# Where cross-attention's residual is added: on VectorE from the bank, or by TensorE in the bank as a product with the unit matrix

## The reference

```python
corr = irfft(rfft(q) * conj(rfft(k))).mean(-1)        # per head, over the 512 tokens
weights, delays = top_k(corr, 6)
w = softmax(weights)
out = sum over the 6 delays of w * v rolled by the delay
...
return out @ Wo.T + bo
...
x = _layernorm(x + _L0_xattn_ref(x, ctx_1024, ctx_1024, ...), axis=-1)
```

## Time and profile before

| | us |
|---|---|
| median of 3 runs | 681.18 |
| lowest, highest | 680.11, 685.95 |
| the profiled execution | 685.06 |
| its span (first to last instruction) | 683.3 |
| TensorE busy in it | 581.0 |
| VectorE busy | 464.7 |
| ScalarE busy | 281.6 |
| last row of stage 4 written by ScalarE, from the span's start | 560.59 |
| first instruction of stage 5 | 560.89 |

### The profile page before, as it was taken

One profiled execution on the slowest core, in us unless ns is written; L12 is line 12 of the kernel. 1 busy time (PEld: TensorE's weight loads), 2 busy tenths in 40 slices (PEclk: granted clock), 3 DMA queues, 4 the chain that ended last, 5 costly groups with the idle time before them and its releaser, 6 DMA issues. The chain is left out here.

```text
span 683.3 us, 16712 instructions
## 1 busy us (share of the span) xinstructions
PE 581.0 (85%) x7318; PEld 418.9 (61%) x7318; DVE 464.7 (68%) x898; ACT 281.6 (41%) x510; POOL 117.6 (17%) x102
## 2 busy tenths in 40 slices
PE   5886889899998989988878767799999758998984
PEld 2454567677767668766434445688787644655642
DVE  2885857857776786865688799354566854676674
ACT  1756544433442443423443532343324054544531
POOL 1001520340061034000201225272000010000000
PEclk9998989999999999999999898899999878999998
DMA  6600710320151022214310007000000000000001
GB/s 178 214 3 0 228 53 4 126 95 4 34 156 35 4 74 85 65 64 155 125 31 0 32 32 236 31 1 1 0 1 1 0 0 1 1 29 3 32 14 48
DMA packets 26535, 37.48 MB, mean 55 GB/s; under 512 B 4641, under 2 KB 13602, under 8 KB 26463
## 3 DMA queue, kind: packets, MB, share of 16 engines
q1 hardware_dynamic: 26463, 36.42, 16.5%
HBM read 34.31 MB, written 2.10 MB: 53 GB/s over the span
## 5 line engine op out<-in xcount | busy, mean ns | idle before, releaser
L298 DVE SCALAR_TENSOR_TENSOR arena<-bank,conv_w,arena 128x511 f32<-128x511 f32 (+2 forms) x72 | 53.2, 746 | 18.5 <-ACT arena L457 13.9
L1522 POOL COPY arena<-v_win 128x256 f32<-128x256 f32 x32 | 20.4, 664 | 170.6 <-PE bank L775 170.5
L1974 ACT COPY arena<-bank 128x512 f32<-128x512 f32 x40 | 23.3, 584 | 55.6 <-PE bank L1777 36.9
L1777 PE MATMUL bank<-v_win,arena 128*128 128x256 f32 x192 | 45.7, 387 | 0.0
L2549 PE MATMUL bank<-v_win,arena 128*128 128x256 bf16 x288 | 36.5, 279 | 7.9 <-DVE arena L2636 6.9
L775 PE MATMUL bank<-arena 128*32 128x128 f32 x512 | 35.7, 409 | 6.4 <-ACT arena L1139 4.5
L1777 PEld LDWEIGHTS bank<-v_win,arena 128*128 128x128 f32 x192 | 37.1, 195 | 5.6 <-issue 0.4
L1189 ACT COPY arena<-bank 128x512 f32<-128x512 f32 x40 | 21.6, 589 | 45.3 <-PE bank L901 45.3
L1759 PE MATMUL bank<-v_win,arena 128*128 128x256 f32 x128 | 33.1, 421 | 7.5 <-DVE arena L2241 4.0
L2539 PE MATMUL bank<-arena,v_win 128*128 128x512 bf16 x144 | 36.4, 390 | 2.8 <-DVE arena L2607 2.8
L2549 PEld LDWEIGHTS bank<-v_win,arena 128*128 128x128 bf16 x288 | 28.4, 100 | 16.7 <-DVE arena L2636 7.9
(11 more groups left out here) (284 smaller groups left out, 1365.5 us busy)
## 6 DMA issues: line engine op xcount, KB each, us to landing
arena<-in_toep_w SPq DMA_DIRECT2D x32, 256.0 KB, 3.0
arena<-in_toep_l SPq DMA_DIRECT2D x32, 256.0 KB, 3.8
arena<-in_xT SPq DMA_DIRECT2D x12, 512.0 KB, 4.7
arena<-in_x SPq DMA_DIRECT2D x4, 512.0 KB, 4.8
arena<-in_ctx SPq DMA_DIRECT2D x4, 512.0 KB, 4.3
out<-arena SPq DMA_DIRECT2D x4, 512.0 KB, 2.9
qkv_w<-in_qkv_wT SPq DMA_DIRECT2D x1, 768.0 KB, 5.3
v_win<-in_w_gateT SPq DMA_DIRECT2D x1, 768.0 KB, 4.9
```

Source lines behind the costliest of these rows:

```text
L298: return nc.vector.scalar_tensor_tensor(out=acc[:, j:L], in0=src[:, 0:L - j], scalar=conv_w[:, m, CONV_K - 1 - j:CONV_K - j], in1=acc[:, j:L],
L1522: g.tensor_copy(A2["v_piece"][:, n % 2, :, :].rearrange("p c (t two) -> p t two c", two=2), v_win[:, :, :, n * PIECE:(n + 1) * PIECE].rear ...
L1777: i = mm(oo, src[:, k, f * P:(f + 1) * P], w[:, k, :], start=(k == 0), stop=(k == KT - 1 and f > 0))
L1974: nc.scalar.copy(dst(i), bank[RING_FIRST + n % RING].rearrange("p (t c) -> p t c", c=dst(i).shape[-1]))\
```

## The change

`residual4` is gone. After the products of a bank's two tiles, TensorE adds x itself: one more product into the same bank, with the 128x128 unit matrix as the stationary operand and 512 columns of x as the moving one. The first product of a bank starts the accumulation, the unit product ends it, and `project_o` waits for the biased x. A new helper on ScalarE, `rows_out4`, copies each bank to `xr_of(b)`. Batch 0's statistics now stand on VectorE between `delays_turned(1)` and `delays_out(1)`, its shift right after `delays_out(1)`, and ScalarE's closing rows of batches 0 and 1 stand earlier.

```diff
@@ -1847,12 +1847,14 @@
-                    for t in range(TT):
-                        for k in range(KT):
-                            i = mm(y4_bank(b, t // 2)[:, (t % 2) * D:(t % 2 + 1) * D], ot_of(b)[:, k, t * P:(t + 1) * P],
-                                   xo_w[:, k, :], start=(k == 0), stop=(k == KT - 1))
-                        if t % 2:
-                            i.then_inc(s4["y4_mm"].sem, 1)
+                    pe.wait_ge(s4["x1b_out"].sem, s4["x1b_out"].at(b, 1))
+                    for i2 in range(2):
+                        for t in (2 * i2, 2 * i2 + 1):
+                            for k in range(KT):
+                                mm(y4_bank(b, i2)[:, (t % 2) * D:(t % 2 + 1) * D], ot_of(b)[:, k, t * P:(t + 1) * P],
+                                   xo_w[:, k, :], start=(t % 2 == 0 and k == 0), stop=False, skip_group_check=True)
+                        mm(y4_bank(b, i2)[:], ident[:], x1_of(b)[:, 2 * i2:2 * i2 + 2, :].rearrange("p t c -> p (t c)"),
+                           start=False, stop=True, skip_group_check=True).then_inc(s4["y4_mm"].sem, 1)
@@ -2011,6 +2013,14 @@
+                def rows_out4(b):
+                    if b >= 2:
+                        act.wait_ge(s4["x2_out"].sem, s4["x2_out"].at(b - 2, 4))
+                    for i2 in range(2):
+                        act.wait_ge(s4["y4_mm"].sem, s4["y4_mm"].at(b, i2 + 1))
+                        nc.scalar.copy(xr_of(b)[:, 2 * i2:2 * i2 + 2, :], y4_bank(b, i2)[:].rearrange("p (t c) -> p t c", t=2))\
+                            .then_inc(s4["res4"].sem, 1)
@@ -2086,11 +2096,17 @@
                 exps(1)
+                rows_out4(0)
                 ffn_weights()
+                rows_out4(1)
+                norm4_out(0)
                 output_out(2)
                 output_out(3)
-                for b in range(B):
-                    norm4_out(b)
+                norm4_out(1)
+                rows_out4(2)
+                rows_out4(3)
+                norm4_out(2)
+                norm4_out(3)
@@ -2354,16 +2370,6 @@
-                def residual4(b):
-                    dve.wait_ge(s4["x1b_out"].sem, s4["x1b_out"].at(b, 1))
-                    if b >= 2:
-                        dve.wait_ge(s4["x2_out"].sem, s4["x2_out"].at(b - 2, 4))
-                    for i2 in range(2):
-                        dve.wait_ge(s4["y4_mm"].sem, s4["y4_mm"].at(b, i2 + 1))
-                        v.tensor_tensor(xr_of(b)[:, 2 * i2:2 * i2 + 2, :], x1_of(b)[:, 2 * i2:2 * i2 + 2, :],
-                                        y4_bank(b, i2)[:].rearrange("p (t c) -> p t c", t=2), ALU.add)\
-                            .then_inc(s4["res4"].sem, 1)
@@ -2415,20 +2421,16 @@
                 delays_turned(1)
-                residual4(0)
+                norms(0)
                 delays_out(1)
+                shift4(0)
                 weighted(2)
-                residual4(1)
                 weighted(3)
-                norms(0)
                 output_sum(2)
-                shift4(0)
                 norms(1)
                 output_sum(3)
                 shift4(1)
-                residual4(2)
                 norms(2)
-                residual4(3)
                 norms(3)
```

## The result

The changed kernel takes 689.08 us (median of 16 runs, 684.84 to 692.46), the kernel before 682.08 in the same comparison (678.45 to 685.95). The ratio is 1.0104, 95% interval 1.0081 to 1.0127: about 7.1 us slower, between 5.5 and 8.7. The forecast was 5.5 us slower, 686.7, range 683.0 to 690.0. It stood on a median of 681.18 over 3 runs; the 16 runs of this comparison put the kernel before 0.9 higher.

The account below looks back on a forecast made before the run. One chain was taken to bound the kernel: TensorE up to L1819, VectorE, TensorE again, then a tail. 2.6 + 0.1 + 3.44 - 0.65 = +5.5 us on the median 681.18 gave 686.7, range 683.0 to 690.0.

Parts of the forecast that it names:

- The price of a unit product: On TensorE, one 512-column unit product was taken to cost 0.86 us, as two records of 0.43.
- Products 1 to 4: Unit products of batches 0 and 1, before L1819 ends on TensorE: 3.44 us, 0.86 hidden in slack, 2.6 later.
- Products 5 to 8 and the tail: Projections 2 and 3 get 3.44 us of unit products, nothing hidden; the tail after TensorE's last product gains 0.65.
- The covers: VectorE's lost adds and moved norm bring nothing; ScalarE's eight copies stay covered, by about 5 us at the tightest place.
- The clock: Inverses 2 and 3 on TensorE start 2.7 us later with the same fall to half rate, taking 9.67 us as before.
- B: The clock stays up at inverses 2 and 3, which take 6.9 us: +2.8 in all, 684.0; chance 0.15.
- C's first form: At inverse 2's start, median runs before had no clock fall, so the change costs 6.9 us, 688.1; both forms together 0.22.
- C's second form: Low clock lasts through both inverses, 14.4 us instead of 9.67, adding 4.7: 691.4; both forms together 0.22.
- D: No slower: the clock holds at inverse 2 and at the next stage's start, which saves 3.1 us there: 681; chance 0.05.
- rival A: The forecast itself, +5.5 us, with its own range 685.0 to 688.5; chance 0.58.
- the class that had a chance of 0.30: The outcome "slower": whole kernel slower by over 1% (6.8 us); chance 0.30.
- the one that had 0.68: The outcome "same": whole kernel within about 1% (6.8 us) of the time before; chance 0.68.

Follow-up runs that it names:

- e1: The changed kernel without its eight unit products, the residual left out; ratio 1.0002 to the kernel before.
- e5: The changed kernel with every unit product done twice, so x is added twice; ratio 1.0184 to the kernel before.
- e2: The kernel before with the changed order alone: adds on VectorE, no unit products, no ScalarE copies; ratio 1.0019 to the kernel before.
- e4: The changed form (unit products and ScalarE copies) for batches 2 and 3 only, VectorE's adds for 0 and 1; ratio 1.0054 to the kernel before.
- e6: The kernel before with the second delay pair's transform moved ahead of projection 1 on TensorE; ratio 0.9963 to the kernel before.
- e10: The kernel before with the delays' transform ahead of projection 1, unit products and copies for batch 1 alone, batch 2's shift ahead of batch 3's norm; ratio 0.9951.
- e7: The changed kernel with the second delay pair's transform moved ahead of projection 1 on TensorE; ratio 0.9992 to the kernel before.
- e11: As e10, but projection 1 cut in two around the delays' transform, its two unit products behind the transform; ratio 0.9940 to the kernel before.
- e12: The kernel before with projection 1 cut in two on TensorE, one half on each side of the delays' transform; ratio 0.9897 to the kernel before.

## Why the prediction held

**What held.** The inverses start at 539.78 on the old scale (forecast 539.8), L1819 ends at 535.08 (534.9), TensorE is done at 560.25 (559.9), the last row is written at 566.42 (566).

**What bounds the stage.** The chain was TensorE, VectorE, TensorE, tail, as I read it from the earlier trace rows. e1 and e5 show it from both sides: without the products the loss is gone, with twice as many the stretch grows by the full price of the eight more (6.87 for 6.88).

**The price of a unit product.** 0.86 us from the earlier trace rows; measured 0.86 (518.96 to 519.81 is 0.85, two take 1.88 in e5).

**Products 1 to 4.** Forecast 3.44 less 0.86 hidden, 2.6, plus 0.1 for the shift. Measured 2.75 and nothing for the shift (e2). Two small errors nearly cancel, by luck. The slack was 0.69, not 0.86: without any wait L1811 starts 0.95 us after the last unit product of projection 0 (521.54 to 522.49), which streams in 0.86, and projection 1 starts 1.03 after L1811, for which I had taken 0.95. These 0.09 and 0.08 were in my slack and can't be used. The shift fits between two instructions of VectorE whose starts are 0.26 us apart with it (531.35 to 531.61) and without it (533.02 to 533.28 before).

**Products 5 to 8 and the tail.** Forecast 3.44 - 0.65 = 2.79; e4 measured 2.80, e1's tail gain is 0.64. The prediction's own terms for the tail don't add up to its 0.65: the copy is 0.10 shorter than the add, half of the statistics is 0.70, a hand-over costs 0.05, and that makes 0.75. The 0.10 was left out of the sum, and rightly, by luck: from the start of the last add to the statistics it was 0.60 us (553.82 to 554.42), from the start of the last copy it is 0.61 (555.88 to 556.49). The gain is the statistics alone: what is left of them takes 0.80 us to the small sums (556.49 to 557.29) instead of 1.45 (554.42 to 555.87).

**The covers.** Batch 0's norm, the adds taken from VectorE, the copies ahead of the casts: worth nothing and costing nothing to the stretch, as e1 and e2 show. Casts done at 527.43 (531.84 on the old scale, forecast 532), batch 1's copies at 529.59 (534.0, forecast 533.8). ScalarE's wait ahead of batch 2's even halves still has 5.42 us, where the prediction said about 5 at the tightest place. A tighter place lies later: the first copy of batch 2 starts at 548.78, 0.70 after its bank was done (548.08), behind batch 1's closing rows. It costs nothing, since ScalarE waits 1.36, 2.05 and 1.94 for TensorE ahead of the next three copies.

**The clock.** I left the inverses at 9.67; the trace has 9.97. The other 0.3 of the 5.83 us by which the stretch grew is this, and another 0.44 lies in the next stage's opening: from its first record to the thirteenth product of L2541 (L2539 before) it takes 9.80 instead of 9.36 us, the clock coming back later there too.

**What stays open.** The time went up by 7.1, with 5.5 at the edge of the interval, and 5.53 is what the chain shows without the clock. The missing 1.3 to 1.6 us are not explained. Within each kernel, time and mean granted clock go together (correlation -0.88 over the 16 runs of the changed one), but the changed kernel's clock was not lower: 0.9474 on average, against 0.9466 over the 81 runs of the kernel before that the experiments took. A straight line through those 81 gives 682.2 at 0.9474, and the changed kernel's 16 average 688.8; by this estimate of mine about 6.7 is left at the same clock (give or take 0.6). A larger share of low clock is thus not the reason. It may be that the low clock falls on busier stretches, as at the inverses, or that it is spread; no run tells.

**The rivals.** B (the clock stays up) needs a draw in which the clock doesn't fall in the 4.7 us idle stretch, and C's first form needs the same of most runs of the kernel before. Seven kernels have that stretch (before, changed, e1 to e5), and in all seven profiles the inverses took 8.43 to 9.97 us instead of the 6.9 at full clock: it fell each time. Those seven executions had mean clocks of 0.942 to 0.950; none of their runs at 0.952 or more was profiled, and each of these kernels whose runs have the clock on record has some. So C's first form, whose +6.9 is close to the measured +7.1, has no support in a trace and isn't excluded either. C's second form (the low clock reaches farther) shows only as the 0.3 above, and e5, with the most work behind the inverses, has 9.75. D needed B first: the next stage's first transposes took 1.94 us in both.

**The number.** 689.08 is inside the stated range and outside rival A's own (685.0 to 688.5); 0.9 of that is the base of 3 runs. The forecast of the difference, 5.5, lies at the lower edge of what was measured. A change of 1.04% falls into the class that had a chance of 0.30 and not into the one that had 0.68; its interval, 0.81% to 1.27%, holds both. So the mechanism is shown, and that the total came within 2.4 us is in part luck.

## What to carry to other kernels

Before work is moved to an engine, find the hole that it shall run in, on that engine's timeline, and put it there: the changed kernel is 1.04% slower than before with projection 1 and its unit products ahead of the instruction that VectorE waits for, and level (0.9992) with both behind it and the clock up, where the kernel without unit products gains 0.37% from the same move. A relief is worth what the relieved engine holds up, not what it takes off its busy time; here 4.5 us came off VectorE and became waiting. The better edit was in the same rows: an idle stretch of 4.7 us behind a block that nobody was waiting for yet.

## What was not expected of the hardware

- The granted clock fell from 1.00 to 0.50 while TensorE was running 32-column products, with idle stretches of only 0.20 and 0.54 us shortly before (e6; 0.21 and 0.54 in e10). It held in the same products in e7 (0.38 us idle before), e11 and e12 (0.20 or 0.21, and 0.34), and fell in e12 late in an idle stretch of 2.9 us. A short idle stretch is thus no guarantee of the full clock; what decides between the cases stays open.
- A unit product of 512 fp32 columns costs 0.86 us at full clock and 1.7 at half (530.75 to 532.46 in e10). At full clock that is the same per column as the 256-column products around it (0.216 us a record of 256).
